# A 7x7 convolution over normalised images: another order for the prologue, both seeds in a row, last stores by image

## What is computed

```python
ph = jnp.clip(P[0], -3, 3) + 3;  pw = jnp.clip(P[1], -3, 3) + 3
ih, iw = jnp.floor(ph).astype(jnp.int32), jnp.floor(pw).astype(jnp.int32)
...
for di, dj, frac in corners:
    kern = kern.at[:, cidx, ih + di, iw + dj].add(weight * frac[None], mode='drop')
...
out = jax.lax.conv_general_dilated(gn(x), kern, (1, 1), [(3, 3), (3, 3)], ...)
return x + out + bias[None, :, None, None]
```

## Time and profile before

| | |
|---|---|
| median of 3 runs | 328.8 us (326.24, 328.8, 332.79) |
| the profiled execution | 326.01 us |
| its span on the core | 324.2 us, mean granted TensorE clock 0.962 |
| busy | PE 289.6 us, DVE 273.1, ACT 218.6, POOL 155.0 |
| shifted copies `xb<-xs` | 192 transfers, 4.1 to 4.4 us from issue to landing (median) |
| loads and stores of images | 256 transfers, 2.9 and 5.0 us from issue to landing on SP |

### The profile page before, as it was taken

One profiled execution on the slowest core, in us unless ns is written; L12 is line 12 of the kernel. 1 busy time (PEld: TensorE's weight loads), 2 busy tenths in 40 slices (PEclk: granted clock), 3 DMA queues, 4 the chain that ended last, 5 costly groups with the idle time before them and its releaser, 6 DMA issues.

```text
span 324.2 us, 9588 instructions
## 1 busy us (share of the span) xinstructions
PE 289.6 (89%) x3380; PEld 201.7 (62%) x3380; DVE 273.1 (84%) x454; ACT 218.6 (67%) x327; POOL 155.0 (48%) x259
## 2 busy tenths in 40 slices
PE   5920589999999989999999989999999999999990
PEld 2700466666666657776677766677877666766760
DVE  4489598999898888989899989989998989897331
ACT  2369796967868676967696788778796868461300
POOL 6232545645363727374564527372929274644000
PEclk9975599999999999999999999999999999999997
DMA  8953354989898896979797989999898939489605
GB/s 141 151 110 85 88 140 96 255 196 242 186 217 215 195 236 146 265 167 255 156 259 173 237 189 193 254 189 255 168 260 176 262 78 243 107 223 235 135 12 99
DMA packets 128253, 59.07 MB, mean 182 GB/s; under 512 B 122068, under 2 KB 122068, under 8 KB 128228
## 3 DMA queue, kind: packets, MB, share of 16 engines
q1 hardware_dynamic: 115204, 24.90, 40.9%
q0 software_dynamic: 9312, 33.04, 36.8%
q10 hardware_dynamic: 3712, 0.80, 1.4%
HBM read 12.88 MB, written 12.85 MB: 79 GB/s over the span
## 4 chain that ended last, share of the span: by engine, by line
PE 57%; DVE 9%; SPq 9%; issue 8%; DMA 7%; POOL 3%; ACT 3%; DVEq 0%; ACTq 0%; POOLq 0%
PE ps_s L802 17%; PE ps_x L802 16%; PE ps_y L802 12%; PE ps_eo L802 8%; SPq L196 6%; DMA xraw<-x 4%; DVE e L451 3%; SPq L186 3%; DVE d L451 2%; DMA xb<-xs 2%; DVE xs L472 2%; POOL xn L702 2%; PE ps_eo L770 1%; POOL xb L690 1%; DMA wnat<-L_conv_weight 1%
## 5 line engine op out<-in xcount | busy, mean ns | idle before, releaser
L690 POOL DMA_DIRECT2D xb<-xs x192 | 93.5, 494 | 62.0 <-DVE xs L472 59.3
L802 PE MATMUL ps_s<-xb,w 128*64 128x392 f16 (+1 forms) x576 | 103.4, 329 | 0.9 <-DMA xb<-xs 0.8
L802 PE MATMUL ps_s<-xs,w 128*64 128x392 f16 (+1 forms) x576 | 103.9, 329 | 0.2 <-ACT m L349 0.2
L702 POOL TENSOR_SCALAR xn<-xraw,scale,offset 32x784 f32<-32x784 f32 x32 | 55.0, 1724 | 79.3 <-DVE offset L448 79.3
L802 PEld LDWEIGHTS ps_s<-xs,w 128*64 128x64 f16 x576 | 62.4, 110 | 22.0 <-issue 1.5
L802 PEld LDWEIGHTS ps_s<-xb,w 128*64 128x64 f16 x576 | 62.3, 110 | 9.2 <-DMA xb<-xs 2.2
L802 PE MATMUL ps_x<-xs,w 128*64 128x392 f16 x384 | 66.5, 329 | 0.1
L802 PE MATMUL ps_x<-xb,w 128*64 128x392 f16 x384 | 66.6, 329 | 0.0
L343 ACT ACTIVATE xs<-e 128x900 f16<-128x900 f32 x48 | 59.1, 1230 | 10.3 <-DVE e L451 6.4
L802 PE MATMUL ps_eo<-xb,w 128*64 128x392 f16 (+1 forms) x384 | 65.5, 326 | 0.0
L802 PE MATMUL ps_eo<-xs,w 128*64 128x392 f16 (+1 forms) x384 | 65.5, 326 | 0.0
(11 more groups left out here) (90 smaller groups left out, 403.7 us busy)
## 6 DMA issues: line engine op xcount, KB each, us to landing
xb<-xs POOLq DMA_DIRECT2D x96, 168.8 KB, 4.1
xb<-xs POOLq DMA_DIRECT2D x96, 166.9 KB, 4.4
xraw<-x SPq DMA_DIRECT2D x124, 98.0 KB, 2.9
out<-result SPq DMA_DIRECT2D x124, 98.0 KB, 5.0
xraw<-x ACTq DMA_DIRECT2D x4, 98.0 KB, 3.9
out<-result ACTq DMA_DIRECT2D x4, 98.0 KB, 3.7
wnat<-L_conv_weight POOLq DMA_DIRECT2D x1, 36.0 KB, 3.8
pts<-L_conv_P POOLq DMA_DIRECT2D x2, 1.1 KB, 3.1
```

The costliest lines, as they stand in the source:

```text
L690: pool.dma_start(dst[32 * g:32 * g + 32, 0:run - line * past], src[32 * f:32 * f + 32, line * past:run]).then_inc(shifted[par][b], DMA)
L702: pool.tensor_scalar(xn[96:128, u % 2, :, SLOTS * m:SLOTS * m + ROWS, 1:1 + SIDE // 2], image(u % RING, m)[96:128, :].rearrange("p (n w k) ...
L802: last = pe.matmul(into[p:p + HALF, :, 0:PER * wide], w[:, n // 2, s, q, t, :], moving.rearrange("p n q m -> p n (q m)"), start=fresh and ...
```

## The change

It gives the first two units lists of their own and touches the rest in two places.

- **Loads.** Points and weights are loaded by SP, ahead of the images. The two images of unit 0 have semaphores of their own. SP loads unit 1 after unit 0 has landed; unit 2 is loaded by POOL (8 transfers); SP loads unit 3 after it has issued its share of the shifted copies.
- **Sums and folds.** Images 0 and 1 are summed, folded and squared one by one. The folds stand in other places: both between the fp32 matmuls, `mean(1)` between streams 0 and 1 of unit 0, `variance(1)` ahead of stream 4, `mean(2)` ahead of stream 7, `both_moments(2)` in unit 1 ahead of stream 2, `both_moments(3)` in unit 1 ahead of stream 7. TensorE has 12 matmuls on zeros at the start (8 before) and 20 more ahead of the first stream.
- **Kernel scaling.** Half of `kern` is scaled on ACT. DVE normalises the last group of image 1. `fold` is built from `ident` by four instructions in place of nine.
- **Shifted copies of unit 0.** Streams 0 to 5 are copied in four pieces (0; 1 and 2; 3; 4 and 5), each as soon as it is ready, groups 0 and 2 from SP and 1 and 3 from POOL. Streams 6 to 8 stay one batch on POOL.
- **Outputs of unit 0** stand inside DVE's preparation of units 0 and 1.
- **All later units:** `seed(k=0)` and `seed(k=1)` follow each other, ahead of `sums`. **The last stores** begin for each image when it is done.

```diff
+PIECES = [(0, 1), (1, 2), (3, 1), (4, 2)]
...
         def last_store(queue, first):
-            queue.wait_ge(combined, OUTS * UNITS)
             for m in range(PER):
+                queue.wait_ge(combined, OUTS * UNITS - PER + 1 + m)
                 for g in (first, first + 2):
...
-            load(0, 0, (0, 1))
+            sp.dma_start(pts[:, :, :], P.rearrange("t c (a k) -> (c a) t k", a=CHUNKS)).then_inc(points_loaded, DMA)
+            sp.dma_start(wnat[:, :], weight.rearrange("o c k -> o (c k)")).then_inc(weights_loaded, DMA)
+            fetch(sp, 0, 0, 0, 0)
+            fetch(sp, 0, 0, 0, 1)
+            fetch(sp, 0, 0, 1, 0)
+
+            sp.wait_ge(image_loaded, LOAD // PER)
+            sp.wait_ge(x_loaded[0], loaded(0, 0))
             load(1, 1)
...
-            load(2, 2)
+            sp.wait_ge(ends_zeroed, THIRDS + 1)
+            for n, (s, count) in enumerate(PIECES):
+                sp.wait_ge(hi_ready, s + count)
+                sp.wait_ge(lo_ready, s + count)
+                shift(sp, 0, s, count, (0, 2), piece_shifted[n])
             load(3, 3)
...
-                middle(u, first)
-                seed(u, h, 0, first)
+                middle(u)
+                for k in range(2):
+                    seed(u, h, k)
                 if early:
                     sums(u + 3, (h + 3) % RING, nth)
...
-                seed(u, h, 1, first)
...
-            for h in range(RING):
-                step(h, h, (h + 3) // RING, True, True, True, first=h == 0)
+            high(1, 1, *BATCHES[0], first=True)
+            squares(2, 2)
+            high(1, 1, *BATCHES[1], first=True)
+            sums(3, 3, 0)
+            for batch in BATCHES[2:]:
+                high(1, 1, *batch, first=True)
+            root(2)
+            normalise(2, 2)
+            for h in range(1, RING):
+                step(h, h, (h + 3) // RING, True, True, True)
...
             odd_differences(0, 0)
-            differences(0, 0)
             low(0, 0, *BATCHES[0])
             filter_low(0)
             low(0, 0, *BATCHES[1])
             filter_low(1)
+            filter_sum(2, sums4[:, 2:4], kern[:, 0:2], kern[:, 2:4])
+            differences(0, 0)
             second_differences(0, 0)
...
+            outs_0(0)
+            low(0, 0, *BATCHES[4])
+            filter_low(4)
+            low(0, 0, *BATCHES[5])
+            outs_1(0)
             spread(1)
             rstd(1)
+            outs_2(0, 0, 0)
+            odd_differences(1, 1)
             mean(2)
...
+            differences(1, 1)
+            low(1, 1, *BATCHES[0])
+            low(1, 1, *BATCHES[1])
+            outs_3(0)
...
+            pool.wait_ge(x_loaded[0], loaded(0, 0))
+            for m in range(PER):
+                for g in range(GROUPS):
+                    fetch(pool, 2, 2, m, g)
...
-            mean(1)
-            both_moments(1)
+            warm(6)
+            pe.wait_ge(normalised, NORMS)
+            warm(6)
+            pe.wait_ge(lo_ready, 1)
+            warm(8).then_inc(marked, 1)
...
-            for u in range(2):
-                step(u, u, 0, True, True, first=u == 0)
+            for s in range(NS):
+                if s == 1:
+                    mean(1)
...
+                if s == 4:
+                    variance(1)
+                    pe.wait_ge(seeded, 1)
...
+                if s == 7:
+                    mean(2)
+                    pe.wait_ge(seeded, 2)
+                convolve(0, 0, s, None)
+            for s in range(NS):
...
+                if s == 2:
+                    both_moments(2)
...
+                if s == 7:
+                    both_moments(3)
+                    pe.wait_ge(seeded, 4)
+                convolve(1, 1, s, 0)
```

309 lines of the change are left out of this document (198 added, 111 removed).

## The result

The changed kernel takes 340.55 us (median of 4 executions, 340.01 to 344.36) against 329.37 us for the kernel before (4 executions, 326.24 to 332.79). The ratio is 1.040, 95% interval 1.028 to 1.052: slower. Measured again beside experiment e10 it was 343.92 us, ratio 1.040, interval 1.032 to 1.049. The forecast had the direction and most of the mechanism; its size, 335 us, was 5.5 us short, and the time lies above its range of 331 to 338. Ratios here leave out disturbed executions, of which e4 had two in four and e7 three in four, so that none is given for these two.

What follows compares the result with a forecast made beforehand. TensorE was taken as the bound outside the first stretch, which VectorE feeds. Profiled 326.0 us, plus 7.9 for unit 2 starting later, minus 0.5 for stores, gave 333.4; forecast 335 for the median, range 331 to 338.

Steps and rivals of the forecast that it cites:

- Up to the first low half: Start of unit 0: offset at 14.5 us, bounds 13.4 and 16.5, and the first difference at 17.5.
- Last low half of unit 0: VectorE's preparation of unit 0: 15.0 us from the first difference, ending at 32.5 instead of 35.36.
- First shifted copies: Unit 0's batch for streams 6 to 8: last issue at 34.0, landing 4.4, stream 6 at 38.4 (bounds 36.5 and 39.7).
- Stream 6 itself: Unit 0 on TensorE: stream 6 takes 1.92 us, so the mean of unit 2 is folded at 40.3.
- Unit 0 to unit 1: First new wait, behind the mean fold of unit 2: 9.4 us of preparation, so unit 1 starts at 49.7.
- Both moments of unit 2: Second new wait, in unit 1: fold at 55.6, chain of 9.1 us, stream 3 at 64.7, then 2.0 for the clock.
- Both moments of unit 3: Fold ahead of unit 1's stream 7 at 74.6, with 2.0 us for the clock; unit 2 starts at 81.1.
- The rest: Later units and ends: seeds cost nothing, last stores save 0.5 us, POOL's loads of unit 2 take 0.95 each, hidden.
- Later units' waits vanish: Rival, units 2 to 15: all 6.9 us of waits gone, giving 326.5 us; chance 0.1.
- The new waits are short: The second rival, units 0 and 1: clock held, landing 2.5, POOL 2.09, giving 326.3 us; chance 0.22.
- POOL's loads are slow: Rival, loads of unit 2: 1.5 to 2.0 us each, first difference 4 to 8 late, 338 to 342 us; chance 0.13.
- The change does what it says: Rival, start-up: the 15 us saved at the first matmul stay saved, giving 319 us; chance 0.05.

Runs made afterwards that it cites:

- e10: Changed kernel with 20 instead of 12 multiplications of zeros at the start; median 345.3 us, ratio 1.048 to the kernel before.
- e4: Changed kernel with mean(2), both_moments(2) and both_moments(3) folded ahead of streams 6, 0 and 4 instead of 7, 2 and 7; median 330.5 us.
- e7: e4 plus POOL's copies of unit 1's streams 3 to 5 before normalising unit 2, and unit 1's middle and seeds earlier on ScalarE; median 332.8 us.
- e5: Changed kernel with zeros multiplied into a free bank in TensorE's waits, nothing moved; median 338.9 us, ratio 1.018 to the kernel before.
- e9: The changed kernel run again, unchanged; median 343.9 us.
- e14: Changed kernel with SP's loads of units 3 and 4 held until unit 0's copies of streams 6 to 8 landed; median 345.0 us, ratio 1.058.
- e11: e7 with zeros multiplied in TensorE's remaining waits; median 326.29 us, ratio 0.992 to the kernel before.
- e12: e11 with 20 instead of 12 multiplications of zeros at the start; median 329.04 us, ratio 0.995 to the kernel before.
- e8: Kernel before with only both seeds in a row and the last stores by image, old prologue; median 328.68 us, ratio 0.994.
- e13: Kernel before with zeros multiplied in TensorE's two waits ahead of unit 0; median 330.6 us, ratio 1.010.

## Why the prediction was half right

The order of the waits, their releasers and the direction were as forecast. What failed is the price of the lower clock in the chain from unit 0 to unit 2: 4.0 us charged, behind two stops, where the fall came behind three, and 6.8 measured by e5. Two smaller terms failed beside it, the start of POOL's copies and POOL's normalisation.

**Up to the first low half: right.** `offset` 14.27 for 14.5, first difference 17.22 for 17.5. The upper bound was not: I took 16.5 for fp32 matmuls all at the lower clock, and in e9 they came to 19.68. I had counted about 2 us for them and left out that each group stands between two steps of the statistics, so that the whole chain stretches.

**Last low half of unit 0: 33.84 for 32.5.** I had put 0.4 us for VectorE's waits. It had 0.56 and 0.80 for ScalarE and 0.50 for TensorE's bank.

**First shifted copies: the landing right, the issue late.** The last issue started at 35.86 and not at 34.0: 1.3 from the low half, and 0.6 that POOL took to begin. The landing was 4.31 us for my 4.4. The row of the chain of waits:

```profile
35.86 4.31 DMA xb<-xs
```

So the landing was as priced, but stream 6 started at 40.21 for 38.4, beyond the upper bound of 39.7.

**Stream 6 itself: the largest single miss, and the step that failed.** I wrote that it takes 1.92. I had charged the lower clock behind the two long waits only, and not behind this one of 3.59. The window 40 to 44 reads 0.50 and the stream took 3.7. My second rival had it that "the clock fell within 3 us of idleness"; here it fell in this stop of 3.59, and not in the one of 3.33 ahead of unit 2. The fold of the mean came at 44.0 for 40.3.

**Unit 0 to unit 1: 10.7 for 9.4.** POOL began its issues 0.94 us behind the low half (at 49.90), so that the fourth started 2.4 behind it and not 1.6. Unit 1 started at 54.68 for 49.7.

**Both moments of unit 2: 61.0 for 55.6, the chain 9.8 for 9.1.** POOL's normalisation ran near its full price. Its two images, and the two by themselves (ns, shortest, median, longest):

```profile
62.99 3.51 POOL L808 TENSOR_SCALAR xn<-xraw,scale,offset 32x784 f32<-32x784 f32 x2 [11.10 <-DVE offset L533]
...
L808 POOL TENSOR_SCALAR xn<-xraw,scale,offset x2: 1034/1758/2482, 63.0 to 65.5; 32x784 f32<-32x784 f32 x2
```

The first took 2.48 us, beside two low halves of VectorE (63.06 to 64.76), the second 1.03, with VectorE idle. So VectorE's 1.7 us of low halves cost POOL 1.4, where I had added 0.6 for 1.6. The Trainium skill, "GPSIMD Engine Reference", Specifications, which I had weighed, puts the contention on VectorE's instructions of two SBUF inputs; the low halves are such, and the trace agrees. The full price, 10.0 for the chain, was nearer than my 9.1. TensorE waited 7.58 us ahead of stream 3 for the middle: "some 7 us ahead of stream 3, released by middle" was right.

**Both moments of unit 3: 11.1 us for 9.9.** Streams 3 to 6 behind the long stop ran at 0.50 for the whole of 72 to 76 and not at full rate until after 76; I had charged 2.0 for the clock and 3.2 is what it came to. From that fold to unit 2 it was 6.6 for 6.5.

Added up, the terms missed 7.3 us at unit 2 (88.40 for 81.1): 1.8 for the late issue, 1.9 for stream 6 at the lower clock, 1.3 for unit 1's copies, 0.4 and 1.2 for longer slow stretches, 0.7 for POOL. About half of it is clock (1.9, 0.4 and 1.2): I had charged 4.0 us for it in all, which makes 7.5 by these rows, and e5 measured 6.8. The sum of the forecast, 333.4, missed the profiled execution, 340.47, by 7.1; that 335 missed the median by 5.5 only is luck, since 1.6 had been added for a median above the profile and the two were level.

**The rest: right.** POOL's loads took 5.22 us for eight, 0.65 each and not 0.95, and were hidden. Units 2 to 15 took 242.5 us, the tail 7.8 for 8.1.

**The rivals.** *Later units' waits vanish*: did not happen. *The new waits are short*: no. The clock cost more than priced (6.8 for 4.0), and so did POOL (3.51 for 2.7); the two landings came about as priced, 4.31 for 4.4 and 2.8 for 3.1. The landing of 2.5 that it needed was not reached for these copies even in e14 without the loads beside them (2.8 to 2.9). *POOL's loads are slow*: no. *The change does what it says*: e4 shows what that would take, three folds moved, and that it then only ties, since VectorE has the same work to do before unit 2.

What I had not weighed is that the errors have the same sign. Each stop was priced by itself at its likely size, but a stop can lower the clock, which delays the next fold and all that waits for it. The bounds of such terms belong together on the long side.

## What to carry to other kernels

A start that is earned at the front can be lost before the steady state: here 13 us at the first matmul became at most 0.6 us at unit 2 (72.65 in e11 for 73.24) in every order tried, and a new prologue should be judged by the time at which the steady state begins and not by its first matmul. A small fold or reduction that an in-order engine does between large blocks should stand as early as its inputs allow, since two other engines may be standing behind it: moving three such folds by one to three streams gave back 14 us. Price the lower clock behind every stop of TensorE that the forecast contains and not only behind the longest (in the changed kernel the stop of 3.59 us was followed by a window at 0.50, the one of 3.33 by one at 1.00), and where it is hidden behind another engine, as in the kernel before, expect that it is paid as soon as a result is taken from the slow stretch.

## What the runs showed of the hardware

- The same program ran its fp32 matmuls in two speeds: a group of four of 256 columns in 1.03 to 1.13 us or in 1.91 to 2.08, over 12 us in which TensorE was busy without a break. The granted clock reads 1.00 in both; a window of e9 from that stretch:

```profile
12.00:16.00 4.00, 4.00 (x14) 2.82 (x14) 0.83 (x8) 1.39 (x4) 1.10 (x2) 1.00 1.24 171
```

  So at the start of a program the column of the granted clock does not tell the rate of a matmul; its duration does. Twenty multiplications of zeros ahead gave the faster speed in the two profiles taken (e10, e12), twelve in seven of twelve.
- The rate can also rise in the middle of such fp32 matmuls. In the kernel before, which has eight multiplications of zeros, they begin at the slower rate and end at the faster one, as they do in e8 and e13:

```profile
8.74 2.05 PE L770 MATMUL ps_eo<-cols,diag 96*128 96x256 f32 x4 [1.11 <-DVE cols L574]
...
13.54 1.03 PE L770 MATMUL ps_x<-cols,diag 96*128 96x256 f32 x4
```

  In e9 they stayed at the slower rate to their end at 20.2. No run here shows what decides between the two.
- A GpSimd instruction is slowed by some VectorE instructions and not by others. The two of `xn` took 2.08 us together in the changed kernel at 36.39, beside VectorE's `result` instructions that read `ps_x`, and 1.4 more at 62.99, beside low halves, which read two SBUF tiles.
- Shifted copies of 168.8 KB land in 2.8 to 2.9 us without loads beside them and in 3.5 to 4.1 with them.
- POOL begins to issue copies 0.6 to 0.9 us behind the low half that it waited for (33.84 to 34.41, 48.96 to 49.90 in the changed kernel).
